# A side schedule re-timed: the normalisation two slots later, half of the GELU matrices one slot later, a flip and a projection shifted, and the query rotation rearranged

## The chip, the cores and the metric

The program runs on one core of one Trainium2 chip. Its time is the device time of one launch in microseconds (us); the kernel before took 6043.84 us in the median of three runs (6041.26 to 6050.09). A core has a matrix engine (TensorE, PE in the profile, its weight loads PEld), VectorE (DVE), ScalarE (ACT), GpSimd (POOL) and the queue that issues DMAs (SyncE, SP). Each works through its own instructions strictly in order, and they wait for each other by semaphores.

## The reference

Eight blocks follow each other (a transformer stack with expert layers and recurrences between them). Only the first is touched: six layers over a batch of 16 items of 56 query rows by 128 features, 16 heads of 8, a context of 1500 keys.

```python
for i in range(NL):                          # NL = 6
    xn = _adaln(x, noise_emb, n1_w[i], n1_b[i])          # (x - mean) / std, scaled and shifted per item
    q, k, v = jnp.split(xn @ qkv_w[i].T, 3, axis=-1)
    a = _attn(_rope(q), _rope(k), v, src_mask) @ so_w[i].T      # self attention, 56 keys
    x = x + a
    xn = _adaln(x, noise_emb, n2_w[i], n2_b[i])
    q = _rope(xn @ cq_w[i].T)
    k = _rope(context @ ck_w[i].T)                              # cross attention, 1500 keys
    v = context @ cv_w[i].T
    a = _attn(q, k, v, ctx_mask) @ co_w[i].T
    x = x + a
    xn = _adaln(x, noise_emb, n3_w[i], n3_b[i])
    h = jax.nn.gelu(xn @ f1_w[i].T + f1_b[i], approximate=False)
    x = x + (h @ f2_w[i].T + f2_b[i])
# _rope(x) = [x1 * cos - x2 * sin, x1 * sin + x2 * cos], x1 and x2 the halves of a head
```

## The kernel before

**Slots.** The cross attention is the bulk of the block. It is cut into 6 x 16 = 96 units s (layer and batch item), and each unit into 12 key tiles kt of 125 keys: one pair (s, kt) is a slot. In each slot TensorE forms the scores of 16 heads in two halves (L1561), ScalarE takes their exponentials (L2067), and TensorE multiplies them with the values (L1587). Beside that a slot forms part of the scores of a later unit a first time (L1575), of which VectorE takes row maxima (L1940).

**Keys and queries.** Ahead of its unit each third of a key block (500 keys) is made by two matmuls (L1601) into a PSUM bank. VectorE turns it (a shuffle of the halves, L1821) and multiplies it with the cosines (L1822); the second one frees the bank. GpSimd then multiplies by the sines (L2087), adds (L2091), and, since the scores run in three bfloat16 parts, forms the rest (L2094, after ScalarE's high part, L1966) and the low part (L2097, after ScalarE's middle part, L1970). DMAs carry the parts to the key stack. In `key_gpsimd` these steps stand at the slots +1, +2 and +3 of the key block (`late`). The query goes the same way (L2105, L1976).

**The side work.** Everything else of the layer (the self attention, the norms, the MLP) is for half a batch (8 units) at once and is spread over the 96 slots of these units. Such a stretch is a phase, numbered ph from -1 to 12, and t = 0 to 95 counts its slots. Phases -1 and 12 are the run-up and the end, with little or no scoring. What stands where is set by tables: `T_NORM` (start of the three norms), `T_UP` (which of the four MLP matrices, with their GELUs, at which t), `T_DOWN`, `T_ROPE` (three rotations of queries and keys), `T_SV`, `T_SELF` (eight self attentions, each from t = a: scores at a, transposes `st` at a+2, weighing `sw` a+3, turn a+4, flip a+5, and for each second one a projection at a+7). A norm that starts at t = at has its mean at +0, its variance at +2, and its application by GpSimd in two halves of three instructions each (`norm_gpsimd`), at +3 and +4 (called in `gpsimd`); the matrices that read it stand at +7.

**The banks.** All side work on TensorE writes to three PSUM banks (4, 6, 7), taken in turn by the class `Banks`. A user's bank is its rank in one list, modulo three. The list is written by `fixed_order` (key, value, turn, flip, project, rows), `phase_order` and `self_weigh_order`, slot by slot. A matmul waits until the user three ranks ahead has been read (`side.emptied(...)`, `side.before`), and its reader waits for `side.filled`. So a user that moves within the list shifts the bank of each user that it passes.

**The engines' programs.** For each slot TensorE, VectorE and ScalarE call first `fixed_*`, then `phase_*`; the activation table of ScalarE holds exponential and logarithm (`LN_EXP`), and the GELU needs another, so that ScalarE loads tables around it (L2022, L2025). In a slot GpSimd calls the norm halves before or after the key steps as `gpsimd` has them.

Of the kernel before, what the change touches and what calls it, by code (L numbers as in the profile page):

```python
# [113 lines left out]
def by_batch(a):  # L114
    return a.rearrange("p (b s) -> p b s", s=S)
# [1127 lines left out]
T_UP, T_DOWN, T_ROPE, T_SV = {13: (0, 1, 2, 3)}, 15, {23: 0, 24: 1, 71: 2}, 24  # L1243
# [10 lines left out]
class Block0:  # L1254
# [12 lines left out]
    def __init__(self, k):  # L1267
        self.k = k
        ev = k.events
        with ExitStack() as st:  # L1270
# [24 lines left out]
            self.largest = sb("row_max", [QC, PAIRS, 3])  # L1295
            self.m_part = sb("neg_max_parts", [QC, WIDE], BF16)[:, :]
# [70 lines left out]
        self.rope_turned = Ordered(k, "l0_rope_turned", [(*key, i) for key in ropes for i in range(2)])  # L1367
# [33 lines left out]
    def fixed_order(self, s, kt):  # L1401
# [7 lines left out]
        if 1 <= s <= NS and kt == 3:  # L1409
            order.append(("flip", s - 1))  # L1410
# [11 lines left out]
    def phase_order(self, ph, t):  # L1422
# [16 lines left out]
        if nxt:  # L1439
            for i, a in enumerate(T_SELF(ph)):  # L1440
# [8 lines left out]
                if t == a + 7 and i % 2 == 1:  # L1449
                    order.append(("sproject", ph, i // 2))  # L1450
# [141 lines left out]
    def fixed_tensor(self, e, s, kt):  # L1592
# [27 lines left out]
        if 1 <= s <= NS and kt == 3:  # L1620
# [38 lines left out]
    def phase_tensor(self, e, ph, t):  # L1659
# [48 lines left out]
        for i, a in enumerate(T_SELF(ph)):  # L1708
# [39 lines left out]
            if t == a + 7 and i % 2 == 1:  # L1748
# [29 lines left out]
    def max_parts_vector(self, e, s):  # L1778

        side, key = self.side, ("rows", s)  # L1780
        neg, m = side.bank(*key)[0:QC, BANK - PAIRS:BANK], self.m_part[:, 1:1 + 3 * PAIRS].rearrange(
            "q (p j) -> q p j", j=3)
        e.wait_ge(side.emptied(*key), side.before(*key))
# [56 lines left out]
    def phase_vector(self, e, ph, t):  # L1840
# [18 lines left out]
        if t in T_ROPE:  # L1859
# [4 lines left out]
            bk = side.bank(*key)[:, 0:HALF]  # L1864
# [4 lines left out]
            if n == 1:  # L1869
                e.wait_ge(self.roped.sem, self.roped(ph, 0))  # L1870
            e.scalar_tensor_tensor(out=by_batch(o), in0=by_batch(bk), scalar=scale, in1=cs, op0=ALU.mult,
                                   op1=ALU.mult).then_inc(self.rope_turned.sem, 1)
            e.wait_ge(self.rope_turned.sem, self.rope_turned(ph, n, 0))
            e.stream_shuffle(bk, bk, OTHER_HALF).then_inc(self.rope_turned.sem, 1)
            e.wait_ge(self.rope_turned.sem, self.rope_turned(ph, n, 1))
            e.scalar_tensor_tensor(out=by_batch(bk), in0=by_batch(bk), scalar=scale, in1=sn, op0=ALU.mult,
                                   op1=ALU.mult).then_inc(self.rope_sin.sem, 1)
            e.wait_ge(self.rope_sin.sem, self.rope_sin(ph, n))
            e.tensor_tensor(o, bk, o, ALU.add).then_inc(self.roped.sem, 1)
            e.drain().then_inc(side.emptied(*key), 1)  # L1880
# [1801 lines left out]
```

## Time and profile before

| | |
|---|---|
| median of three runs (range) | 6043.84 us (6041.26 to 6050.09) |
| profiled execution: time, span | 6043.84 us, 6042.0 us |
| PE busy, share of the span, instructions | 5595.8 us, 93%, 55893 |
| PEld | 4177.1 us, 69%, 55893 |
| DVE | 3779.0 us, 63%, 8627 |
| ACT | 3230.0 us, 53%, 6405 |
| POOL | 2247.7 us, 37%, 2204 |

Shares are over the whole span of eight blocks. The span in 40 slices (each digit a tenth of the slice in which the engine is busy; PEclk is the granted clock of TensorE in tenths of full speed) shows the first block in slices 2 to 20:

```profile
PE   5899999999999999999799999998799999989997
ACT  1566666666766766667543344443333333324764
POOL 4666666666666666656200000000011111156440
PEclk7999999999999999999898999999799999998998
```

The costliest groups of the page (line, engine, operation, tensors with partitions x elements, count, then busy us and mean ns, then the engine's idle time just before them and what ended most of it) are the inner loop of the slots. VectorE's maxima waited for TensorE 170 us, ScalarE's exponentials 515 us:

```profile
L1940 DVE TENSOR_REDUCE row_max<-psum 112x1 f32<-112x500 f32 x2304 | 1443.3, 670 | 185.2 <-PE psum L1575 170.4
L2067 ACT ACTIVATE weights<-psum 125x448 f32<-125x448 f32 x2304 | 1140.8, 541 | 521.2 <-PE psum L1561 514.6
L1575 PE MATMUL psum<-key_stack,query_stack 97*128 97x500 bf16 x2304 | 874.6, 380 | 111.0 <-DMA query_stack<-query_parts 51.1
L1561 PE MATMUL psum<-query_stack,key_stack 121*128 121x112 bf16 x9216 | 837.6, 213 | 33.2 <-ACT weights L2067 27.9
```

### The profile page before, as it was taken

The page shows a single profiled execution, that of the slowest core. Times are in us where ns is not written, and L with a number is a line of the kernel's source. Part 1 is how long each engine was busy: PE and PEld are TensorE (multiplying, and loading weights), DVE is VectorE, ACT ScalarE, POOL GpSimd, SP SyncE. Part 2 cuts the span into 40 slices and gives each one's busy share as a digit, 9 for nine tenths or more (in the row PEclk, how much of TensorE's full clock was granted, in tenths as well). Part 3 has the DMA queues.
Part 4 walks back from the last instruction along what each step waited for, and adds up shares of the span by engine and source line. Part 5 has one row for each costly group of instructions (what it writes and reads, how often), then busy time and mean ns, then how long its engine had stood idle before and what let it go on. Part 6 is the DMA issues. An engine that isn't in the chain of part 4 may idle for free.

```text
span 6042.0 us, 140669 instructions
## 1 busy us (share of the span) xinstructions
PE 5595.8 (93%) x55893; PEld 4177.1 (69%) x55893; DVE 3779.0 (63%) x8627; ACT 3230.0 (53%) x6405; POOL 2247.7 (37%) x2204
## 2 busy tenths in 40 slices
PE   5899999999999999999799999998799999989997
PEld 4667667677676676776457778776477777756984
DVE  3888888887887888888553444444544444444553
ACT  1566666666766766667543344443333333324764
POOL 4666666666666666656200000000011111156440
PEclk7999999999999999999898999999799999998998
DMA  2776776776767767768400100001000000030000
GB/s 63 120 118 106 119 120 104 120 116 107 125 110 115 121 109 116 121 107 130 92 11 10 42 32 32 30 29 33 11 11 16 11 16 11 11 105 24 1 1 25
DMA packets 396485, 407.85 MB, mean 68 GB/s; under 512 B 125575, under 2 KB 372946, under 8 KB 393786
## 3 DMA queue, kind: packets, MB, share of 16 engines
q1 hardware_dynamic: 395834, 398.85, 37.6%
q8 instruction: 447, 7.32, 0.6%
q14 instruction: 204, 1.67, 0.1%
HBM read 158.00 MB, written 0.46 MB: 26 GB/s over the span
## 4 chain that ended last, share of the span: by engine, by line
PE 62%; POOL 8%; SPq 7%; DVE 7%; issue 7%; ACT 5%; DMA 3%; POOLq 1%; DVEq 0%; ACTq 0%
PE psum L2276 11%; PE psum L2243 10%; PE psum L1575 5%; PE psum L1587 4%; PE psum L2288 4%; PE psum L1561 4%; SPq L1475 4%; POOL slot_context L3476 3%; PE psum L1723 2%; PE psum L1609 2%; PE psum L1601 2%; SPq L1493 2%; PE psum L416 2%; PE psum L430 2%; DVE row_max L1940 2%
## 5 line engine op out<-in xcount | busy, mean ns | idle before, releaser
L1940 DVE TENSOR_REDUCE row_max<-psum 112x1 f32<-112x500 f32 x2304 | 1443.3, 670 | 185.2 <-PE psum L1575 170.4
L2067 ACT ACTIVATE weights<-psum 125x448 f32<-125x448 f32 x2304 | 1140.8, 541 | 521.2 <-PE psum L1561 514.6
L1575 PE MATMUL psum<-key_stack,query_stack 97*128 97x500 bf16 x2304 | 874.6, 380 | 111.0 <-DMA query_stack<-query_parts 51.1
L1561 PEld LDWEIGHTS psum<-query_stack,key_stack 121*128 121x128 bf16 x9216 | 654.1, 99 | 370.9 <-issue 184.6
L1561 PE MATMUL psum<-query_stack,key_stack 121*128 121x112 bf16 x9216 | 837.6, 213 | 33.2 <-ACT weights L2067 27.9
L2356 DVE TENSOR_REDUCE l_stat<-psum 128x1 f32<-128x1500 f32 (+1 forms) x224 | 391.7, 1749 | 544.9 <-PE psum L2243 544.9
L2276 PE MATMUL psum<-l_ctx_v,l_turned 125*128 125x128 f32 x5376 | 713.7, 281 | 16.4 <-ACT l_turned L2314 12.2
L2276 PEld LDWEIGHTS psum<-l_ctx_v,l_turned 125*128 125x128 f32 x5376 | 643.1, 191 | 59.2 <-ACT l_turned L2314 40.2
L1587 PE MATMUL psum<-weights,values 125*17 125x112 f32 x18432 | 553.9, 261 | 0.0
L1587 PEld LDWEIGHTS psum<-weights,values 125*17 125x17 f32 x18432 | 408.0, 97 | 144.1 <-issue 141.2
L2314 ACT ACTIVATE l_turned<-psum 125x512 f32<-125x512 f32 x448 | 251.3, 597 | 434.9 <-PE psum L2288 432.1
L2097 POOL TENSOR_TENSOR key_parts<-key_temp,key_parts 128x500 bf16<-128x500 f32 x288 | 327.2, 1136 | 420.0 <-ACT key_parts L1970 420.0
L2087 POOL TENSOR_TENSOR key_temp<-key_temp,rope_sin 128x500 f32<-128x500 f32 x288 | 360.4, 1252 | 280.3 <-DVE key_temp L1821 280.3
L2973 POOL MEMSET l_turned<- 125x128 f32 x2 | 0.4, 216 | 1169.1 <-DVE x_state L796 1169.1
L2288 PE MATMUL psum<-ident,l_weights 128*125 128x128 f32 (+1 forms) x2800 | 400.6, 276 | 19.4 <-ACT l_keys L2823 8.0
L2094 POOL TENSOR_TENSOR key_temp<-key_temp,key_parts 128x500 f32<-128x500 f32 x288 | 328.3, 1140 | 233.6 <-ACT key_parts L1966 233.6
L2288 PEld LDWEIGHTS psum<-ident,l_weights 128*125 128x125 f32 (+1 forms) x2800 | 348.8, 185 | 83.0 <-issue 39.4
L2091 POOL TENSOR_TENSOR key_temp<-key_temp 128x500 f32<-128x500 f32 x288 | 358.2, 1244 | 42.4 <-POOL key_temp L2087 1.7
L2339 ACT ACTIVATE l_weights<-psum,l_stat 128x1500 f32<-128x1500 f32 (+1 forms) x224 | 344.0, 1536 | 38.1 <-DVE l_stat L2356 38.1
L2837 POOL TENSOR_TENSOR l_ctx_v<-l_ctx_v,l_ctx_w 125x512 f32<-125x512 f32 x48 | 61.0, 1272 | 786.0 <-DVE l_ctx_v L2831 786.0
L1575 PEld LDWEIGHTS psum<-key_stack,query_stack 97*128 97x128 bf16 x2304 | 224.1, 97 | 173.4 <-DMA query_stack<-query_parts 72.5
L2243 PE MATMUL psum<-l_keys,l_q 128*128 128x389 f32 x896 | 314.9, 493 | 4.2 <-ACT l_weights L2339 3.6
(539 smaller groups left out, 10182.9 us busy)
## 6 DMA issues: line engine op xcount, KB each, us to landing
key_stack<-key_parts SPq DMA_DIRECT2D x1728, 125.0 KB, 4.6
ctx_t<-in_ctxT SPq DMA_DIRECT2D x96, 750.0 KB
l_ctx_v<-in_ctxV SPq DMA_DIRECT2D x32, 750.0 KB
query_stack<-query_parts SPq DMA_DIRECT2D x576, 28.0 KB, 3.5
l_ctx_t<-in_ctxT SPq DMA_DIRECT2D x16, 750.0 KB
slot_context<-in_ctxV SPq DMA_DIRECT2D x16, 750.0 KB
key_stack<-ctx_mask_rows SPq DMA_DIRECT2D x576, 3.9 KB
sm_w<-in_sm_w SPq DMA_DIRECT2D x3, 2048.0 KB
```

The lines of the kernel that those rows point to most:

```text
L1561: mm = e.matmul(self.k.psum[:, h, (p % 4) * QC:(p % 4 + 1) * QC], ks[:, at:at + 128], q[:, p * QC:(p + 1) * QC])
L1575: e.matmul(self.k.psum[:, 2 + n % 2, 0:500], q[0:ROWS_MAX, p * QC:p * QC + 128], ks[0:ROWS_MAX, p, c * 500:(c + 1) * 500]).then_inc(self.m ...
L1587: mm = e.matmul(self.k.psum[32 * j:32 * j + 17, 5, g * QC:(g + 1) * QC], v[:, kt, p, :], w[:, p * QC:(p + 1) * QC], start=kt == 0 and g == ...
L1940: e.tensor_reduce(self.largest[:, i % PAIRS, i // PAIRS:i // PAIRS + 1], k.psum[0:QC, 2 + i % 2, 0:500], AX.X, ALU.max, negate=True).then_ ...
L2067: e.activation(half(self.p[kt % RING_P], h), self.k.psum[0:KN, h, 0:HALF], ACT.Exp).then_inc(self.exped.sem, 1)
L2087: e.tensor_tensor(tm[:, 1, :], tm[:, 1, :], self.sin[:, c * 500:(c + 1) * 500], ALU.mult).then_inc(self.key_turned_sin.sem, 1)
L2091: e.tensor_tensor(tm[:, 0, :], tm[:, 0, :], tm[:, 1, :], ALU.add).then_inc(self.key_rotated.sem, 1)
L2243: mm = e.matmul(k.psum[:, c, 0:self.step], q[:, r * 128:(r + 1) * 128], self.keys(b)[:, c * self.step:(c + 1) * self.step])
L2276: mm = e.matmul(k.psum[:, 6, 0:128], pt[:, t, :], v[:, t, :], start=t == 0, stop=t == self.tiles - 1)
L2288: tr = e.transpose(bk[0:rows, t * 128:(t + 1) * 128], self.p[j % 2][:, c0:c0 + rows], k.ident[:, :])
L2339: e.activation(self.p[i % 2].rearrange("p (c n) -> p c n", c=self.n_s), k.psum[:, 0:self.n_s, 0:self.step], ACT.Exp, bias=stat[:, 1:2], ac ...
L2356: e.tensor_reduce(self.stat[i % 4][:, 1:2], k.psum[:, 0:self.n_s, 0:self.step], AX.XY, ALU.max, negate=True).then_inc(self.max_ready.sem, 1)
```

## The change

Six edits, all in the first block:

1. `T_UP` spreads the four MLP matrices over two slots (two at t = 13, two at t = 14), and the exponential's table is loaded back after the second and after the fourth GELU.
2. The negated row maximum and what is subtracted from it lie in a tile of their own in SBUF instead of a corner of a side bank, and VectorE no longer waits for that bank before it.
3. The cross attention's head flip moves from kt = 3 to kt = 4, on TensorE, on ScalarE and in the list of banks.
4. The self attention's projection moves from a+7 to a+6, on TensorE, on VectorE and in the list of banks.
5. The rotation first shuffles from PSUM into the idle half of the scratch `k.sq`, then multiplies from PSUM by the cosines, which frees the bank; the product with the sines and the sum read and write SBUF, and the drain is gone.
6. GpSimd's two halves of a norm move from +3 and +4 to +5 and +6.

```diff
-T_UP, T_DOWN, T_ROPE, T_SV = {13: (0, 1, 2, 3)}, 15, {23: 0, 24: 1, 71: 2}, 24
+T_UP, T_DOWN, T_ROPE, T_SV = {13: (0, 1), 14: (2, 3)}, 15, {23: 0, 24: 1, 71: 2}, 24
...
+            self.neg = sb("neg_max", [QC, PAIRS])[:, :]
...
-        self.rope_turned = Ordered(k, "l0_rope_turned", [(*key, i) for key in ropes for i in range(2)])
+        self.rope_turned = Ordered(k, "l0_rope_turned", ropes)
...
# fixed_order; the same in fixed_tensor and fixed_scalar
-        if 1 <= s <= NS and kt == 3:
+        if 1 <= s <= NS and kt == 4:
             order.append(("flip", s - 1))
...
# phase_order; the same in phase_tensor and phase_vector
-                if t == a + 7 and i % 2 == 1:
+                if t == a + 6 and i % 2 == 1:
                     order.append(("sproject", ph, i // 2))
...
# max_parts_vector
-        side, key = self.side, ("rows", s)
-        neg, m = side.bank(*key)[0:QC, BANK - PAIRS:BANK], self.m_part[:, 1:1 + 3 * PAIRS].rearrange(
-            "q (p j) -> q p j", j=3)
-        e.wait_ge(side.emptied(*key), side.before(*key))
+        neg, m = self.neg, self.m_part[:, 1:1 + 3 * PAIRS].rearrange("q (p j) -> q p j", j=3)
...
# phase_vector, rotation
-            bk = side.bank(*key)[:, 0:HALF]
+            bk, other = side.bank(*key)[:, 0:HALF], half(k.sq, 1 - c)
...
+            e.stream_shuffle(other, bk, OTHER_HALF).then_inc(self.rope_turned.sem, 1)
             e.scalar_tensor_tensor(out=by_batch(o), in0=by_batch(bk), scalar=scale, in1=cs, op0=ALU.mult,
-                                   op1=ALU.mult).then_inc(self.rope_turned.sem, 1)
-            e.wait_ge(self.rope_turned.sem, self.rope_turned(ph, n, 0))
-            e.stream_shuffle(bk, bk, OTHER_HALF).then_inc(self.rope_turned.sem, 1)
-            e.wait_ge(self.rope_turned.sem, self.rope_turned(ph, n, 1))
-            e.scalar_tensor_tensor(out=by_batch(bk), in0=by_batch(bk), scalar=scale, in1=sn, op0=ALU.mult,
+                                   op1=ALU.mult).then_inc(side.emptied(*key), 1)
+            e.wait_ge(self.rope_turned.sem, self.rope_turned(ph, n))
+            e.scalar_tensor_tensor(out=by_batch(other), in0=by_batch(other), scalar=scale, in1=sn, op0=ALU.mult,
                                    op1=ALU.mult).then_inc(self.rope_sin.sem, 1)
+            e.wait_ge(side.emptied(*key), side.after(*key))
             e.wait_ge(self.rope_sin.sem, self.rope_sin(ph, n))
-            e.tensor_tensor(o, bk, o, ALU.add).then_inc(self.roped.sem, 1)
-            e.drain().then_inc(side.emptied(*key), 1)
+            e.tensor_tensor(o, o, other, ALU.add).then_inc(self.roped.sem, 1)
...
# phase_scalar
-            if f == 3:
+            if f % 2 == 1:
                 e.preload_act_table_set(LN_EXP)
...
# gpsimd
-                    if layer is not None and t - at - 3 in range(2):
-                        self.norm_gpsimd(e, name, ph, layer, t - at - 3)
+                    if layer is not None and t - at - 5 in range(2):
+                        self.norm_gpsimd(e, name, ph, layer, t - at - 5)
```

Lines move with the edits: L1561 becomes L1562 and so on for TensorE; in the programs of ScalarE and GpSimd all lines are three lower.

The first place is GpSimd around the cross norm of phase 5. `x_normed` is the normalised state, three instructions a half; `key_temp` and `key_parts` are the steps of key blocks. Before:

```order
L2097 TENSOR_TENSOR key_parts<-key_temp,key_parts 128x500
L2121 TENSOR_TENSOR x_normed<-ln_deviation 128x224
L2124 TENSOR_TENSOR x_normed<-x_normed,adaln_scale_shift 128x224
L2126 TENSOR_TENSOR x_normed<-x_normed,adaln_scale_shift 128x224
L2121 TENSOR_TENSOR x_normed<-ln_deviation 128x224
L2124 TENSOR_TENSOR x_normed<-x_normed,adaln_scale_shift 128x224
L2126 TENSOR_TENSOR x_normed<-x_normed,adaln_scale_shift 128x224
L2087 TENSOR_TENSOR key_temp<-key_temp,rope_sin 128x500
L2091 TENSOR_TENSOR key_temp<-key_temp 128x500
L2094 TENSOR_TENSOR key_temp<-key_temp,key_parts 128x500
L2097 TENSOR_TENSOR key_parts<-key_temp,key_parts 128x500
L2105 TENSOR_TENSOR query_block<-l_q,head_parity 128x112
```

After:

```order
L2094 TENSOR_TENSOR key_parts<-key_temp,key_parts 128x500
L2084 TENSOR_TENSOR key_temp<-key_temp,rope_sin 128x500
L2088 TENSOR_TENSOR key_temp<-key_temp 128x500
L2118 TENSOR_TENSOR x_normed<-ln_deviation 128x224
L2121 TENSOR_TENSOR x_normed<-x_normed,adaln_scale_shift 128x224
L2123 TENSOR_TENSOR x_normed<-x_normed,adaln_scale_shift 128x224
L2091 TENSOR_TENSOR key_temp<-key_temp,key_parts 128x500
L2118 TENSOR_TENSOR x_normed<-ln_deviation 128x224
L2121 TENSOR_TENSOR x_normed<-x_normed,adaln_scale_shift 128x224
L2123 TENSOR_TENSOR x_normed<-x_normed,adaln_scale_shift 128x224
L2094 TENSOR_TENSOR key_parts<-key_temp,key_parts 128x500
L2102 TENSOR_TENSOR query_block<-l_q,head_parity 128x112
```

Both halves stood ahead of the next key block's first product; now that block's two products come first, then half one, the rest, half two and the low part.

The second place is TensorE in slot 44 of phase 3. L1601 is the key block (`l_w_context`), L1732 the seven transposes of the self weights (`self_p`) into two banks, four and three, and L1753 the projection (`self_attended`). Before:

```order
L1561 MATMUL psum<-query_stack,key_stack 128x112 x4
L1575 MATMUL psum<-key_stack,query_stack 128x500
L1601 MATMUL psum<-ctx_t,l_w_context 128x500
L1732 MATMUL psum<-ident,self_p 56x128 x7
L1561 MATMUL psum<-query_stack,key_stack 128x112 x4
L1575 MATMUL psum<-key_stack,query_stack 128x500
L1561 MATMUL psum<-query_stack,key_stack 128x112 x4
L1575 MATMUL psum<-key_stack,query_stack 128x500
L1587 MATMUL psum<-weights,values 17x112 x16
L1652 MATMUL psum<-self_pt,self_v 17x112 x8
L1753 MATMUL psum<-self_attended,l_w_attend 128x112
L1561 MATMUL psum<-query_stack,key_stack 128x112 x4
```

After:

```order
L1562 MATMUL psum<-query_stack,key_stack 128x112 x4
L1576 MATMUL psum<-key_stack,query_stack 128x500
L1602 MATMUL psum<-ctx_t,l_w_context 128x500
L1754 MATMUL psum<-self_attended,l_w_attend 128x112
L1733 MATMUL psum<-ident,self_p 56x128 x7
L1562 MATMUL psum<-query_stack,key_stack 128x112 x4
L1576 MATMUL psum<-key_stack,query_stack 128x500
L1562 MATMUL psum<-query_stack,key_stack 128x112 x4
L1576 MATMUL psum<-key_stack,query_stack 128x500
L1588 MATMUL psum<-weights,values 17x112 x16
L1653 MATMUL psum<-self_pt,self_v 17x112 x8
L1562 MATMUL psum<-query_stack,key_stack 128x112 x4
```

In these rows a slot begins with its scores (L1561). The projection has moved from the end of slot 45 to slot 44, between the key block and the transposes. With three banks in turn, the key block, the projection and the first four transposes now take one each, and the last three transposes take the key block's again.

The third place is ScalarE at the MLP matrices of a phase. The GELUs write `l_qd`, the exponentials `weights`. Before:

```order
L1957 ACTIVATE sums<-psum 128x224
L2022 ACT_TABLE_LOAD
L2022 ACTIVATE l_qd<-psum,l_bias 128x448 x4
L2025 ACT_TABLE_LOAD
L2067 ACTIVATE weights<-psum 125x448 x2
L1966 ACTIVATE key_parts<-key_temp 128x500
L1976 ACTIVATE query_parts<-query_block 128x112
L1987 ACTIVATE values<-psum 125x32x16
L2067 ACTIVATE weights<-psum 125x448 x2
```

After:

```order
L1954 ACTIVATE sums<-psum 128x224
L2019 ACT_TABLE_LOAD
L2019 ACTIVATE l_qd<-psum,l_bias 128x448 x2
L2022 ACT_TABLE_LOAD
L2064 ACTIVATE weights<-psum 125x448 x2
L1963 ACTIVATE key_parts<-key_temp 128x500
L1973 ACTIVATE query_parts<-query_block 128x112
L1984 ACTIVATE values<-psum 125x32x16
L2019 ACT_TABLE_LOAD
L2019 ACTIVATE l_qd<-psum,l_bias 128x448 x2
L2022 ACT_TABLE_LOAD
L2064 ACTIVATE weights<-psum 125x448 x2
```

Two of the GELUs, with a table load ahead and one behind, now stand after the next slot's exponentials and after the copies for key (`key_parts`), query (`query_parts`) and values.

## Rows read from the trace of the kernel before

**Rows 1.** A window: from:to, us, busy of PE PEld DVE ACT POOL, PEclk, DMA share, GB/s.

```profile
182.00:2924.00 2742.00, 2605.29 (x37126) 1896.23 (x37126) 2261.74 (x5128) 1862.88 (x4042) 1699.67 (x1693) 1.00 0.73 116
```

**Rows 2.** TensorE's waits, 200 to 2800: total us, times, longest.

```profile
PE psum L1575 <- DMA query_stack<-query_parts: 41.6, 28, 3.4
PE psum L1575 <- DVE row_max L1940: 30.1, 44, 1.4
PE psum L1561 <- ACT weights L2067: 25.3, 32, 1.0
...
PE psum L1575 <- DMA key_stack<-key_parts: 3.2, 11, 0.3
```

**Rows 3.** Timeline, MLP norm, phase 4: start, us, engine, line, tile, [idle before <-releaser].

```profile
1145.22 0.66 POOL L2121 TENSOR_TENSOR x_normed<-ln_deviation 128x224 f32<-128x224 f32 x1
...
1147.12 1.14 POOL L2094 TENSOR_TENSOR key_temp<-key_temp,key_parts 128x500 f32<-128x500 f32 x1
...
1148.30 0.62 ACT L1970 ACTIVATE key_parts<-key_temp 128x500 bf16<-128x500 f32 x1 [0.51 <-POOL key_temp L2094]
...
1151.46 3.52 PE L1681 MATMUL psum<-x_normed,l_w_mlp 128*128 128x448 f32 x8
```

**Rows 4.** The same timeline, tables and GELUs of ScalarE.

```profile
1151.97 1.28 ACT L2022 ACT_TABLE_LOAD   x1
...
1153.27 2.38 ACT L2022 ACTIVATE l_qd<-psum,l_bias 128x448 f32<-128x448 f32 x4
...
1155.66 1.28 ACT L2025 ACT_TABLE_LOAD   x1
...
1157.56 0.37 PE L1561 MATMUL psum<-query_stack,key_stack 121*128 121x112 bf16 x4 [0.45 <-ACT weights L2067]
...
1158.52 0.60 ACT L1987 ACTIVATE values<-psum 125x512 f32<-125x512 f32 x1
```

**Rows 5.** Timeline, phase 5, norm and rotation of the cross attention, then a later slot.

```profile
1541.06 0.73 DVE L1821 STREAM_SHUFFLE key_temp<-psum 128x500 f32<-128x500 f32 x1
...
1544.68 1.24 POOL L2087 TENSOR_TENSOR key_temp<-key_temp,rope_sin 128x500 f32<-128x500 f32 x1
...
1547.07 1.02 PE L1698 MATMUL psum<-x_normed,l_w_attend 128*128 128x448 f32 x2
1547.35 0.62 ACT L1966 ACTIVATE key_parts<-key_temp 128x500 bf16<-128x500 f32 x1 [3.12 <-POOL key_temp L2091]
...
1549.03 0.36 PE L1561 MATMUL psum<-query_stack,key_stack 121*128 121x112 bf16 x4 [0.94 <-ACT weights L2067]
...
1551.62 0.38 PE L1575 MATMUL psum<-key_stack,query_stack 97*128 97x500 bf16 x1 [0.57 <-DVE row_max L1940]
...
1570.58 0.38 PE L1575 MATMUL psum<-key_stack,query_stack 97*128 97x500 bf16 x1 [1.38 <-DMA query_stack<-query_parts]
```

**Rows 6.** The same timeline, first and last instruction of the rotation on VectorE.

```profile
1548.12 0.62 DVE L1871 SCALAR_TENSOR_TENSOR l_q<-psum,rope_cos 128x448 f32<-128x448 f32 x1 [0.38 <-PE psum L1698]
...
1550.12 0.62 DVE L1879 TENSOR_TENSOR l_q<-psum,l_q 128x448 f32<-128x448 f32 x1
```

**Rows 7.** Timeline, slot 44 of phase 3.

```profile
1003.82 1.00 PE L1601 MATMUL psum<-ctx_t,l_w_context 128*128 128x500 f32 x2
...
1004.67 0.93 PE L1732 MATMUL psum<-ident,self_p 128*56 128x128 f32 x7
...
1005.43 0.36 PE L1561 MATMUL psum<-query_stack,key_stack 121*128 121x112 bf16 x4
1005.49 0.66 DVE L1822 TENSOR_TENSOR key_temp<-psum,rope_cos 128x500 f32<-128x500 f32 x1
...
1007.62 0.47 PE L1753 MATMUL psum<-self_attended,l_w_attend 128*128 128x112 f32 x2
```

**Rows 8.** TensorE's timeline in phase 5.

```profile
1382.08 0.60 PE L1575 MATMUL psum<-key_stack,query_stack 97*128 97x500 bf16 x1 [2.01 <-DMA query_stack<-query_parts]
```

**Rows 9.** The window behind that wait, columns as in rows 1.

```profile
1381.80:1385.20 3.40, 3.12 (x17) 2.75 (x18) 1.36 (x2) 1.05 (x2) 1.57 (x3) 0.50 1.08 138
```

More of the change, by code:

```diff
@@ L1619, in fixed_tensor @@
             tr.then_inc(side.filled, 1)
-        if 1 <= s <= NS and kt == 3:
+        if 1 <= s <= NS and kt == 4:
             key = ("flip", s - 1)
@@ L1747, in phase_tensor @@
                 e.transpose(side.bank(*key)[:, 0:TALL], self.so_tall, k.ident[0:TALL, 0:TALL]).then_inc(side.filled, 1)
-            if t == a + 7 and i % 2 == 1:
+            if t == a + 6 and i % 2 == 1:
                 key = ("sproject", ph, i // 2)
@@ L1900, in phase_vector @@
                 self.divide(e, ("sturn", ph, i), self.sinv, self.so, self.s_inverted, self.s_inverted(ph, i))
-            if t == a + 7 and i % 2 == 1:
+            if t == a + 6 and i % 2 == 1:
                 key, m = ("sproject", ph, i // 2), c * (BH // 2) + i // 2
@@ L1989, in fixed_scalar @@
                          ACT.Copy).then_inc(side.emptied(*key), 1)
-        if 1 <= s <= NS and kt == 3:
+        if 1 <= s <= NS and kt == 4:
             key, b = ("flip", s - 1), s - 1
```

## The prediction

> **What bounds the kernel now.** I read the engines' busy shares first, then the window of the stage that the change touches, then what TensorE waits for there, then single slots in order of time. All edits lie in the first block, whose scoring runs from 182 to 2924 us. TensorE is busy 2605.3 of those 2742.0 us [rows 1]; the other engines leave far more. So the stage is TensorE's instruction stream laid end to end, plus 136.7 us of holes: about 11.6 us in each of its nearly twelve phases of 96 slots (a slot is one of the 12 key tiles of one batch item). Its waits are short: for query rows that a DMA brings, for VectorE's row maxima, for ScalarE's exponentials, now and then for key rows [rows 2]. Three things follow. An edit can win at most what it takes out of those holes. A faster side engine wins nothing elsewhere. And every new wait of TensorE counts in full unless the next hole swallows it. In all of the stage TensorE has no wait of weight for a normalised state, for a key block's bank or for a head flip, the three things that the change re-times.
>
> **The later normalisation, MLP.** GpSimd now does its two halves (three instructions each) in slots +5 and +6 instead of +3 and +4, and the consumer's slot is still +7. GpSimd works in order, so both halves stand behind all three steps of the key block (two products and sums, rest, low part). Before, in phase 4: a half takes 1.90 us (1145.22 to the next start at 1147.12), and TensorE starts the up-projection at 1151.46 without waiting [rows 3]. Now: ScalarE's middle copy waited 0.51 us for GpSimd's rest and could start at 1147.79; with its 0.62 us the low part runs from 1148.45 to 1149.6. Then two halves, 3.85 us: 1153.5. TensorE comes at 1151.46, so it waits 2.05 us. Eleven phases inside the stage: **+22.6 us**. The key block is ready 1.7 us earlier, but TensorE did not wait for it here.
>
> **The split up-projection.** Two of the four matrices move a slot later, and the load back to the exponential's table now follows each pair, so there are four loads a phase instead of two. Before, ScalarE loads for 1.28 us, four GELUs take 2.38, the load back ends at 1156.94, and TensorE loses 0.45 us in the next slot and some 0.5 in the fourth matrix [rows 4]. Now, counted from the first matrix: load back done at 3.43, the next slot's two exponentials, key, query and value copies at 5.6 (the value copy of 1158.52 ends 2.2 us after the load did [rows 4]); the fourth matrix needs the bank of that value copy. TensorE has by 4.35 done two matrices (half of 3.52), the next slot's own matmuls (about 1.7) and the third matrix (0.88), so it waits 1.3 us. Against 0.95 lost before: +0.3 us, 11 phases, 3.3 us. Behind the scoring the last phase has nothing beside it: two more loads, 2.6 us. Together **+5.9 us**; bounds -0.95 (no wait left) and +2.6 (both loads in full) per phase.
> The GELUs start at 1153.27, 0.02 us behind the end of the load (1151.97 + 1.28), and TensorE has its exponential 0.6 us behind the end of the load back, which is about the length of that exponential [rows 4]: a load costs its 1.28 us and no more.
> The Trainium skill ("ScalarE: Activation LUTs", What ACT_TABLE_LOAD costs) puts a drain of about 1.38 us on ScalarE beside each load; this case's trace does not agree [rows 4]. By that page an estimate would be 24 more loads at 1.38, 33 us more of ScalarE's time, and 9 us more in the sum if a quarter of it reached TensorE.
>
> **The later normalisation, before the rotations.** Self and cross attention of each phase have the same four lines of order; I take the cross one. Before: both halves ran ahead of the next key block, whose shuffle had ended at 1541.79; that block started only at 1544.68, and TensorE lost 0.94 us to exponentials stuck behind it [rows 5]. Now: the key block's two products (1.25 each) run 1541.8 to 1544.35, half one to 1546.25, rest (1.14) to 1547.4, half two to 1549.35. TensorE stood ready at 1547.07: it waits 2.35 us. The 0.94 us is no gain, because behind the rotation VectorE sets the pace: TensorE waits 0.57 us for a row maximum anyway [rows 5], and the self site ends likewise. What is late next is therefore VectorE's chain, which is shifted whole and shortened only by the quicker rotation.
> The rotation: four instructions from 1548.12 to 1550.74, about 0.67 apart [rows 6], become four, of which the second and third no longer wait for the one before, and the drain goes. A like-sized instruction out of SBUF is unseen beside GpSimd; I take equal durations and 0.25 us saved each, bounds 0 and 0.6.
> Self: two rotations in the chain, 2.35 - 0.5 = 1.85, times 11 phases, **+20.4 us**. Cross: 2.35 - 0.25 = 2.1, less what later holes swallow. GpSimd and the DMAs behind it are no later than now, so the wait for the query's rows, 1.38 us in this phase [rows 5], shrinks; it is not there in each phase (waits of this kind are 28 in the stage, at several places [rows 2]), so I count 0.8 of it, and 0.2 of the key rows' wait of 0.3 [rows 2]: 1.1 left, times 11, **+12.1 us**. The same order in the run-up delays the first keys: +3 us, bounds 0 and 5.
>
> **The moved flip and projection.** They change nothing that TensorE waits for, but each takes one of three rotating banks. In slots 28, 36, 40, 44 and 52 of a phase one bank user now stands between the key block and the turned self weights, so the last three transposes (in slot 52 the first four) land in the key block's own bank and must wait until VectorE has multiplied it. Slot 44: key product at 1003.82, transposes from 1004.67, next scores at 1005.43, hence 0.11 each and the fifth at 1005.11; VectorE is done with the bank at 1005.49 + 0.66 = 1006.15 [rows 7]. That is 1.05 us, +0.1 for the signal, minus what now stands in between, 0.15 (flip) or 0.25 (projection, half of the 0.47 in [rows 7]): 1.0, 0.9, 1.0, 0.9. Slot 52: 1.05 + 0.44 + 0.1 - 0.4 = 1.2. Sum 5.0 us a phase, no hole behind to swallow it: **+55 us** over 11 phases; bounds 3.5 and 6.
> The maxima's negation moves from PSUM to SBUF: five tiny instructions, no wait of TensorE behind them: 0, bounds -0.1 and +0.05 a row.
>
> **The clock.** After a hole of 2.01 us the granted clock fell to 0.50 (1.2 of 2.4 GHz) for the 3.4 us from 1381.8 on [rows 8, 9], 1.7 us of progress lost. There will be 33 new holes of 2.05 to 2.35 us. None or all give 0 to 56 us; half of them, and half of the loss hidden behind VectorE's chain: **+15 us**.
> The sum is 22.6 + 5.9 + 20.4 + 12.1 + 3 + 55 + 15 = 134 us on the profiled execution, whose span is 6042.0 and whose time, 6043.84, is also the median. 6178; I round down to **6172 us**, as overlaps are likelier to eat than to add.
>
> **Rivals.** (a) Half of the bank waits and norm waits are swallowed by holes I counted as local (0.9 us in slots 34, 46): 6044 + 68 = 6112. For: ScalarE and GpSimd get time in each. Against: those holes hang on the same slot's copies. (b) GpSimd and VectorE disturb each other: two of a rotation's instructions now read two SBUF operands; if each waits on the mean half of a 1.25 us GpSimd instruction at GpSimd's busy share of 62% (1699.7 of 2742.0 us [rows 1]), that is 0.39, times 2, times 33 = 25 us more: 6200. No instruction pair of the kind in this block shows it or excludes it.
> The Trainium skill ("SBUF — State Buffer", Who interferes with whom) says that a VectorE instruction with two SBUF inputs and a GpSimd one that reads SBUF exclude each other for their whole length; rival (b) is that rule, and no row here bears on it.
> (c) The other side, faster: the later halves win. If they are done before TensorE reaches the rotation, the 0.94 us here and its twin at the self site, the DMA's 0.8 and three rotations' 0.25 go: -3.4 times 11 = -37, and without the bank waits 6007. It decides from GpSimd's low part ending 2.4 us sooner than I have it; against it stand 7.5 us of GpSimd work between 1541.8 and the rotation. (d) The change does not move the banks as I counted them, and the transposes find another bank: 6172 - 55 = 6117. Its chance stands with (a)'s. Against it: the bank of each user is its rank in one list, and I counted it through a phase.
>
> **Chances.** As worked out 0.63, its own range 6130 to 6215; (a) and (d) 0.17; (b) 0.12; (c) 0.08, of which half ends under 6032. A measurement here tells apart about 0.2% (12 us). Range 6090 to 6220. Faster 0.05, same 0.03, slower 0.92.
>
> **What would show it.** TensorE's wait list gains three entries that it does not have: matmuls of the up-projection and of the rotation for GpSimd's normalised state (near 68 us together, [rows 2] had none) and transposes for VectorE's key product (near 55 us). ScalarE's wait for the key sum at the rotation, 3.12 us [rows 5], is down to a few tenths. Table loads in the stage double. Wrong would be: no wait for the normalised state, or transposes that start as early as 0.85 us after the key product as in [rows 7].

## The result: 3.7% slower, and outside the range

The changed kernel takes 6272.59 us in the median of four runs (6262.12 to 6280.45), the kernel before 6046.97 us beside it (6041.26 to 6052.37): the ratio is 1.0372, 95% interval 1.0353 to 1.0391, or some 226 us. The prediction said 6172 us (6090 to 6220). Its sign was right and so were most of its waits; it had 128 us of the 226. The profiled execution took 6286.42 us (span 6284.6), that of before 6043.84.

The stage from the first exponentials of the scoring to the last is 2781.0 us long before and 3011.4 us now. A window over it, first of the kernel before, then of the changed one (from:to, length, busy of PE PEld DVE ACT POOL, PEclk, DMA share, GB/s):

```profile
182.00:2963.00 2781.00, 2641.00 (x37764) 1921.47 (x37768) 2280.28 (x5170) 1889.24 (x4097) 1699.67 (x1693) 1.00 0.72 114
```

```profile
182.60:3194.00 3011.40, 2716.51 (x37765) 1973.53 (x37769) 2391.54 (x5170) 1936.02 (x4119) 1704.42 (x1693) 0.97 0.67 106
```

These two rows split the loss. TensorE's holes grow from 140.0 to 294.9 us, by 155. Its busy time grows by 75.5 us with the same matmuls: that is the clock, which is down to 0.97 on the mean. In the clock record the time at 0.50 in the stage is 26 us before and 172 us now, and half of the difference, 73 us, is nearly all of the longer busy time. VectorE is busy 111 us longer with as many instructions.

TensorE's waits in the changed kernel (200 to 2980 us), beside [rows 2]:

```profile
PE psum L1576 <- DVE row_max L1937: 65.7, 44, 4.0
PE psum L1733 <- DVE key_temp L1820: 47.2, 55, 1.1
PE psum L1639 <- DVE neg_max_parts L1791: 46.3, 35, 2.2
PE psum L1576 <- DMA query_stack<-query_parts: 38.3, 30, 3.4
PE psum L1699 <- POOL x_normed L2123: 25.7, 22, 1.2
PE psum L1682 <- POOL x_normed L2123: 15.9, 10, 1.8
PE psum L1682 <- ACT values L1984: 15.3, 10, 2.4
```

The second, fifth, sixth and seventh rows are the waits of the prediction: transposes for the key block's bank, matmuls for the normalised state, the fourth MLP matrix for the value copy. The normalised state has 41.6 us where the prediction had near 68: the rotations wait 1.17 us each, not 2.35, for a reason that the experiments show below. The third row is new and was not forecast, and the first has doubled from 30.1 us. The banks can be seen in one place (slot 36 of phase 4, the case of [rows 7]): key product, projection, four transposes, then 0.73 us of waiting for VectorE's product, and three more:

```profile
1315.92 1.40 PE L1602 MATMUL psum<-ctx_t,l_w_context 128*128 128x500 f32 x2
1317.16 0.37 PE L1754 MATMUL psum<-self_attended,l_w_attend 128*128 128x112 f32 x2
1317.37 0.60 PE L1733 MATMUL psum<-ident,self_p 128*56 128x128 f32 x4
1318.70 0.51 PE L1733 MATMUL psum<-ident,self_p 128*56 128x128 f32 x3 [0.73 <-DVE key_temp L1820]
```

**What was not forecast.** The chain that negates the row maximum, slot 34 of phase 4, with GpSimd beside it (timeline of both engines):

```profile
1302.18 1.25 POOL L2088 TENSOR_TENSOR key_temp<-key_temp 128x500 f32<-128x500 f32 x1 [0.43 <-POOL key_temp L2084]
...
1302.64 0.18 DVE L1783 TENSOR_REDUCE neg_max<-row_max 112x8 f32<-112x24 f32 x1
...
1302.85 0.61 DVE L1785 CAST neg_max_parts<-neg_max 112x8 bf16<-112x8 f32 x1
...
1303.38 1.69 POOL L2160 TENSOR_TENSOR l_qd<-l_q,head_of_feature 128x896 f32<-128x896 f32 x1
1303.50 1.60 DVE L1787 TENSOR_TENSOR neg_max<-neg_max,neg_max_parts 112x8 f32<-112x8 f32 x1
...
1305.03 1.13 POOL L2091 TENSOR_TENSOR key_temp<-key_temp,key_parts 128x500 f32<-128x500 f32 x1
1305.13 1.07 DVE L1789 CAST neg_max_parts<-neg_max 112x8 bf16<-112x8 f32 x1
1306.23 0.18 DVE L1791 TENSOR_TENSOR neg_max_parts<-neg_max,neg_max_parts 112x8 bf16<-112x8 f32 x1
...
1306.55 0.28 PE L1639 MATMUL psum<-ident_bf,neg_max_parts 112*72 112x112 bf16 x1 [2.23 <-DVE neg_max_parts L1791]
```

Read the ends. The CAST of eight columns ends at 1303.46, GpSimd's sum at 1303.43. GpSimd has begun its next instruction, which ends at 1305.07; the TENSOR_TENSOR ends at 1305.10. The second CAST ends at 1306.20, GpSimd's third instruction at 1306.16. A chain that takes 1.02 us where nothing holds it takes 3.8 us, because between two of VectorE's short instructions GpSimd gets in with its next one. Over the whole execution 94 of the 96 first CASTs start beside a GpSimd instruction, and all 94 end 32 to 41 ns behind its end; before, with the chain in PSUM, none of the 96 took over 0.18 us. The reduction (L1783) is never longer than 0.18 us, whatever GpSimd does.

The rotation of the keys, same phase, in the same way; two instructions that take 0.63 and 0.62 us in PSUM ([rows 6] has the like of the second) take 1.64 and 1.92:

```profile
1274.15 1.24 POOL L2088 TENSOR_TENSOR key_temp<-key_temp 128x500 f32<-128x500 f32 x1
1274.23 1.64 DVE L1873 SCALAR_TENSOR_TENSOR ln_square<-ln_square,rope_sin 128x448 f32<-128x448 f32 x1
...
1275.35 2.06 POOL L2160 TENSOR_TENSOR l_qd<-l_q,head_of_feature 128x896 f32<-128x896 f32 x1
1275.97 1.92 DVE L1877 TENSOR_TENSOR l_k<-l_k,ln_square 128x448 f32<-128x448 f32 x1
1277.82 2.61 DVE L1937 TENSOR_REDUCE row_max<-psum 112x1 f32<-112x500 f32 x4
1278.63 0.37 PE L1576 MATMUL psum<-key_stack,query_stack 97*128 97x500 bf16 x1 [4.02 <-DVE row_max L1937]
```

It holds the other way round too: GpSimd's instruction at 1275.35 begins while VectorE has the sine product and takes 2.06 us instead of 1.69. TensorE waits 4.02 us for the row maxima queued behind the rotation, once a phase.

The two rotations of queries are not held in this kernel: each takes 2.42 us instead of 2.62, near the 0.25 us that the prediction saved; the rotation of the keys takes 4.74 us instead of 2.61, in all eleven phases.

The Trainium skill ("SBUF — State Buffer", Who interferes with whom) states this rule: VectorE and GpSimd share a port pair as an exclusive lock; an instruction with two SBUF inputs against a reading GpSimd instruction takes it, a copy in a two-port mode takes it, a reduction never does. The durations agree in all three (1.60 us, 0.61 to 1.07 us, 0.18 us); no view shows which mode a CAST ran in.

### The profile page after: what moved, and what is told of

It is laid out like the page before. It is cut to its first block, busy times and chain, and to the rows that moved or that the text cites. A ratio compares the mean times of both kernels' runs of the same rounds, so it can differ in the third digit from the quotient of the medians.

```text
span 6284.6 us, 140597 instructions
## 1 busy us (share of the span) xinstructions
PE 5678.5 (90%) x55893; PEld 4239.4 (67%) x55893; DVE 3890.6 (62%) x8627; ACT 3279.5 (52%) x6429; POOL 2252.9 (36%) x2204
## 4 chain that ended last, share of the span: by engine, by line
PE 62%; DVE 9%; POOL 9%; issue 7%; SPq 5%; ACT 5%; DMA 3%; POOLq 1%; DVEq 0%; ACTq 0%
PE psum L2273 10%; PE psum L2240 9%; PE psum L1576 5%; PE psum L1562 4%; PE psum L1588 4%; PE psum L2285 4%; PE psum L1610 3%; PE psum L1724 3%; POOL slot_context L3473 3%; SPq L1476 3%; PE psum L1602 2%; PE psum L416 2%; PE psum L430 2%; DVE row_max L1937 2%; SPq L1494 1%
## 5 line engine op out<-in xcount | busy, mean ns | idle before, releaser
L1576 PE MATMUL psum<-key_stack,query_stack 97*128 97x500 bf16 x2304 | 889.4, 387 | 146.0 <-DVE row_max L1937 70.9
L1562 PEld LDWEIGHTS psum<-query_stack,key_stack 121*128 121x128 bf16 x9216 | 658.7, 100 | 347.9 <-issue 160.9
L1562 PE MATMUL psum<-query_stack,key_stack 121*128 121x112 bf16 x9216 | 849.3, 215 | 7.4 <-ACT weights L2064 2.1
L2273 PE MATMUL psum<-l_ctx_v,l_turned 125*128 125x128 f32 x5376 | 713.6, 281 | 16.1 <-ACT l_turned L2311 12.1
L1610 PEld LDWEIGHTS psum<-l_w_context,ctx_t 128*125 128x125 f32 x2304 | 316.8, 198 | 10.4 <-issue 1.3
```

The source lines that it names most:

```text
L1562: mm = e.matmul(self.k.psum[:, h, (p % 4) * QC:(p % 4 + 1) * QC], ks[:, at:at + 128], q[:, p * QC:(p + 1) * QC])
L1576: e.matmul(self.k.psum[:, 2 + n % 2, 0:500], q[0:ROWS_MAX, p * QC:p * QC + 128], ks[0:ROWS_MAX, p, c * 500:(c + 1) * 500]).then_inc(self.m ...
L1610: mm = e.matmul(side.bank(*key)[0:KN, i * 128:(i + 1) * 128], self.ctx_t[b % 2][:, t * KN:(t + 1) * KN], self.wk[b // B % 2][:, 1, :])
L2273: mm = e.matmul(k.psum[:, 6, 0:128], pt[:, t, :], v[:, t, :], start=t == 0, stop=t == self.tiles - 1)
```

## The experiments

Each kernel is the kernel before with the named edits, unless it says otherwise. "Holes" is the stage's length less TensorE's busy time, both from a window over the stage as above; "slow" the time at 0.50 of the clock in it. Differences are against before (2781.0, 140.0, 2641.0, 26). The ratio compares medians; the other columns come from one profiled execution of each kernel, that of before at 6043.84 us, where the medians beside the runs were 6047 to 6052, so they can differ from the ratio by some 10 us. Half of "slow" agrees with the longer busy time within 12 us in each row; where the rest comes from (11 us in `without_rope`, 8 in `neg_reduce`) stays open.

| kernel | edits | ratio (95%) | stage | holes | busy | slow |
|---|---|---|---|---|---|---|
| changed | 1-6 | 1.0372 (1.0353-1.0391) | +230 | +155 | +76 | +146 |
| neg_alone | 2 | 1.0229 (1.0214-1.0244) | +142 | +58 | +84 | +170 |
| neg_reduce | 2, CASTs as reductions | 1.0057 (1.0040-1.0074) | +41 | +23 | +19 | +22 |
| rope_alone | 5 | 1.0097 (1.0063-1.0131) | +68 | +33 | +35 | +82 |
| banks_alone | 3, 4 | 1.0087 (1.0070-1.0104) | +60 | +49 | +11 | +9 |
| norm_alone | 6 | 1.0136 (1.0121-1.0151) | +90 | +52 | +38 | +84 |
| norm4_alone | 6 at +4 | 1.0062 (1.0047-1.0077) | +41 | +11 | +30 | +65 |
| up_alone | 1 | 1.0034 (1.0022-1.0046) | +17 | +15 | +2 | +5 |
| timing_only | 1, 3, 4, 6 | 1.0257 (1.0242-1.0273) | +148 | +105 | +43 | +80 |
| without_neg | 1, 3-6 | 1.0294 (1.0279-1.0309) | +174 | +123 | +51 | +107 |
| without_rope | 1-4, 6 | 1.0345 (1.0324-1.0366) | +201 | +132 | +69 | +115 |
| short_steps | none, GpSimd cut | 0.9958 (0.9944-0.9972) | -19 | -33 | +15 | +15 |
| short_neg | 2, GpSimd cut | 0.9980 (0.9969-0.9991) | +0 | -23 | +23 | +32 |

**The negation alone.** The diff is that of `max_parts_vector` in the change.

> The kernel before, with only the maximum's negation moved to SBUF (edit 2). Theory P (VectorE and GpSimd exclude each other): the first CAST takes the rest of the GpSimd instruction that runs when it starts, on average 0.5 to 0.6 us over its 0.17, the whole chain of five about 1.0 us longer; TensorE's transposes of neg_max_parts wait near 40 us in the stage; 6044 + 45 = 6090 us (6070 to 6110). Rival Q (the chain is late only because the norm's halves moved): CAST near 0.17 us, 6044 within 12 us.

Measured 1.0229, 135 us between the medians: Q falls, and P's mechanism stands with three times its price. The five instructions' durations (min/median/max ns):

```profile
L1783 DVE TENSOR_REDUCE neg_max<-row_max x91: 167/178/180, 205.1 to 2994.4; 112x8 f32<-112x24 f32 x91
L1785 DVE CAST neg_max_parts<-neg_max x91: 322/768/1476, 205.3 to 2994.6; 112x8 bf16<-112x8 f32 x91
L1787 DVE TENSOR_TENSOR neg_max<-neg_max,neg_max_parts x91: 166/168/1600, 206.1 to 2995.4; 112x8 f32<-112x8 f32 x91
L1789 DVE CAST neg_max_parts<-neg_max x91: 177/179/1067, 206.3 to 2995.6; 112x8 bf16<-112x8 f32 x91
L1791 DVE TENSOR_TENSOR neg_max_parts<-neg_max,neg_max_parts x91: 176/179/1161, 206.5 to 2995.8; 112x8 bf16<-112x8 f32 x91
```

The holes it makes are 58 us, near P; the other 84 are slow clock, which P left out. In slots 34 and 46 of a phase TensorE waits 1.8 and 1.7 us for the chain (mean of twelve phases), and these slots are 2.5 us longer; in slots 22 and 70 it waits 1.2 us each.

**The CASTs as reductions.**

```diff
-        e.tensor_copy(m[:, :, 0], neg).then_inc(self.negated.sem, 1)
+        e.tensor_reduce(m[:, :, 0], neg.unsqueeze(2), AX.X, ALU.min).then_inc(self.negated.sem, 1)
...
-        e.tensor_copy(m[:, :, 1], neg).then_inc(self.negated.sem, 1)
+        e.tensor_reduce(m[:, :, 1], neg.unsqueeze(2), AX.X, ALU.min).then_inc(self.negated.sem, 1)
```

> As neg_alone, but both CASTs are made as a TENSOR_REDUCE over one element, so that of the five instructions only the two TENSOR_TENSORs read two SBUF operands and none is a plain copy. Theory P1 (only the copy and the two-operand forms wait for GpSimd; the first of them in the chain pays for the running GpSimd instruction): both reductions take 0.17 to 0.2 us, the first TENSOR_TENSOR takes the rest of GpSimd's instruction, 0.5 to 0.8 us, and the time is that of neg_alone or up to 20 us less. P2 (any SBUF operand beside GpSimd is slow): the reductions grow too. P3 (only the copy waits): all five near 0.18 us and the time within 12 us of before.

```profile
L1785 DVE TENSOR_REDUCE neg_max_parts<-neg_max x95: 168/169/171, 200.8 to 2985.7; 112x8 bf16<-112x8 f32 x95
L1787 DVE TENSOR_TENSOR neg_max<-neg_max,neg_max_parts x95: 166/550/1258, 201.0 to 2985.9; 112x8 f32<-112x8 f32 x95
L1789 DVE TENSOR_REDUCE neg_max_parts<-neg_max x95: 167/168/172, 201.6 to 2986.1; 112x8 bf16<-112x8 f32 x95
L1791 DVE TENSOR_TENSOR neg_max_parts<-neg_max,neg_max_parts x95: 176/389/1414, 201.8 to 2986.3; 112x8 bf16<-112x8 f32 x95
```

P1 is right on each instruction: the same data in the same tile, read by a reduction, costs nothing beside GpSimd, and the wait passes to the next TENSOR_TENSOR. P2 and P3 fall. P1's time was wrong: with two instructions instead of four that can meet GpSimd the cost is 34 us, not 115 to 135. What fell most is the slow clock, from 170 us to 22.

**GpSimd's steps cut, without and with the negation in SBUF.**

```diff
-                e.tensor_tensor(tm[:, 0, :], tm[:, 0, :], tm[:, 1, :], ALU.add).then_inc(self.key_rotated.sem, 1)
+                e.tensor_tensor(tm[:, 0, 0:4], tm[:, 0, 0:4], tm[:, 1, 0:4], ALU.add).then_inc(self.key_rotated.sem, 1)
...
-                e.tensor_tensor(part[:, 2, :], tm[:, 1, :], part[:, 1, :], ALU.subtract).then_inc(self.key_lo.sem, 1)
+                e.memset(part[:, 2, :], 0).then_inc(self.key_lo.sem, 1)
```

> The kernel before with GpSimd's key steps cut short: sine product, sum and rest work on 4 of 500 columns, and the low part is a MEMSET (it only writes SBUF). So the scores are not the reference's. It is the control for the next one. GpSimd's busy time in the stage falls from 1700 us to some 700; TensorE's stream is the same, its waits for key rows and exponentials behind the rotation shrink: 5990 to 6045 us.

> short_steps with the negation in SBUF (edit 2). Theory P: the chain now starts beside no GpSimd instruction that reads much of SBUF, so CAST and TENSOR_TENSOR take 0.17 to 0.2 us in most of the 96 chains, and the time is that of short_steps within 15 us, where the same edit on the kernel before cost 135 us. A CAST that begins beside the MEMSET tells whether a writing instruction holds it as well. Rival (SBUF tiles are slower for these instructions by themselves, or the missing wait for the bank moves something): 60 to 135 us over short_steps.

The control took 6023.61 us, the other 6041.42: the edit costs 18 us here and 135 us with GpSimd's work in place. Its first CAST:

```profile
L1785 DVE CAST neg_max_parts<-neg_max x95: 177/179/547, 194.3 to 2938.7; 112x8 bf16<-112x8 f32 x95
```

So the chain is slow because of what GpSimd does beside it, not because of SBUF. The 18 us are 3 over what P allowed; 44 of the 96 first CASTs still start beside what is left of GpSimd's work, most of them just before its end, and 11 are held, for 0.53 to 0.55 us in all. No CAST met a MEMSET, so whether a GpSimd instruction that only writes holds it stays open.

**The rotation alone.** The diff is that of the rotation in the change.

> The kernel before, with only the rotation rearranged through SBUF (edit 5). Theory P: one of the three sine products and the sum of the key rotation meet a GpSimd instruction and grow by 0.9 and 1.3 us, the other ones keep 0.62; TensorE waits about 1.5 us a phase more for row maxima behind the key rotation: 6044 + 15 = 6059 us (6045 to 6075). Rival Q (equal durations, 0.25 us saved for each rotation): 6036 to 6044 us.

Measured 1.0097, about 60 us (from 40 to 80 by the interval): Q falls, P is again right in kind and low in price. Slot 26, from its first score to that of the next slot, grows from 5.47 to 10.15 us on the mean of eleven phases. TensorE waits 3.8 us there, where it waited 1.41. The list of waits puts nine of these eleven under key rows:

```profile
PE psum L1575 <- DMA key_stack<-key_parts: 35.0, 9, 3.9
```

But the timeline shows P's wait, for the row maximum behind the rotation (phase 4):

```profile
1218.58 1.92 DVE L1879 TENSOR_TENSOR l_k<-l_k,ln_square 128x448 f32<-128x448 f32 x1
1220.42 2.77 DVE L1939 TENSOR_REDUCE row_max<-psum 112x1 f32<-112x500 f32 x4
1221.23 0.45 PE L1575 MATMUL psum<-key_stack,query_stack 97*128 97x500 bf16 x1 [3.89 <-DMA key_stack<-key_parts]
```

In each of the eleven phases TensorE starts 0.15 us behind the end of the first of these row maxima, as it does in the kernel before and in the changed kernel; a signal of the key rows' DMA falls within 0.1 us of that start in ten of them, eight times after it, so the list's name for these waits is not what ended them. P also left out that the last sum of the query rotations meets GpSimd here: it takes 1.6 us in 20 of 22, and such a rotation 3.4 us instead of 2.62. In the changed kernel, with the norm's halves later, it is not held.

**Flip and projection alone.** `kt == 3` to `kt == 4` and `a + 7` to `a + 6`, as in the change.

> The kernel before, with only the flip and the projection moved (edits 3 and 4). Theory as in the prediction: the self attention's transposes wait 0.7 to 1.1 us for VectorE's key product in five slots of a phase, 47 us in the stage, the slots grow by 5.0 us a phase: 6044 + 57 = 6101 us (6085 to 6115). Rival (other holes swallow half): 6072 us.

Measured 1.0087, 6102.67 us where 6101 was expected, or 51 us over the runs of before beside it (6051.9) where 57 was. The wait is the one forecast, 55 times (five a phase), and the rival falls:

```profile
PE psum L1732 <- DVE key_temp L1822: 47.1, 55, 1.1
```

**The later halves alone, by two slots and by one.** `t - at - 3` to `t - at - 5`, and to `t - at - 4`.

> The kernel before, with only the norm's halves two slots later (edit 6). Theory as in the prediction: TensorE waits for the normalised state 2.05 us at the MLP matrices and 2.35 us at both rotations, 22.6 + 20.4 + 12.1 + 3 us and some 10 us of slower clock: 6044 + 68 = 6112 us (6090 to 6130). Rival (the waits are 1.05 to 1.6 us, as in the changed kernel, and are so by themselves): 6044 + 35 = 6079 us.

```profile
PE psum L1698 <- POOL x_normed L2126: 50.9, 22, 2.3
PE psum L1681 <- POOL x_normed L2126: 19.9, 11, 1.8
```

Measured 1.0136, some 82 us. The waits are those of the prediction: 22 of 2.31 us at the rotations (2.35 forecast), 11 of 1.81 at the MLP matrices (2.05); the rival falls. The holes of the stage grow by 52 us, where the prediction had 22.6 + 20.4 + 12.1 = 55.1. The slow clock is 38 us, not 10.

> The kernel before, with the norm's halves one slot later instead of two (+4, +5). If GpSimd's order alone decides: at the MLP matrices the second half ends near 1151.3 on the timeline of before, where TensorE comes at 1151.46, and at the rotations the key block's first product runs between the halves, which end at 1547.2 where TensorE comes at 1547.07; no wait over 0.3 us for the normalised state and 0.5 us less wait for exponentials at both rotations: 0.998 to 1.000 of before. Rival (any later half costs): 1.005 or more.

```profile
PE psum L1575 <- DVE row_max L1940: 44.3, 43, 2.0
...
PE psum L1681 <- POOL x_normed L2126: 9.3, 10, 0.9
...
PE psum L1698 <- POOL x_normed L2126: 4.8, 21, 0.2
```

Wrong: 1.0062. It is the rival's figure. At the rotations the wait is 0.2 us as expected, but at the MLP matrices 0.9, and what is won on the exponentials' 0.94 us [rows 5] comes back elsewhere: TensorE's wait for exponentials falls from 25.3 us [rows 2] to 5.1, that for row maxima rises from 30.1 to 44.3, and 14.1 us for the normalised state are new. The sum of the holes is only 11 us more, and 30 us are slow clock.

**The split up-projection alone.** The diff is that of `T_UP` and of the load back.

> The kernel before, with only the split up-projection (edit 1). As in the prediction: +3.3 us in the scoring, +2.6 us behind it, 6044 to 6060 us, within 0.3% of before. Rival (the wait for the value copy in the fourth matrix, 15.3 us in the stage of the changed kernel, is all new time): 1.0025 to 1.004.

```profile
PE psum L1681 <- ACT values L1987: 19.9, 11, 2.2
```

Measured 1.0034, 20 us: the rival. The fourth matrix waits 1.8 us a phase (1.3 forecast), and what was to be saved against it is not there: slots 13 to 15 together are 1.4 us longer, where the prediction had 0.3.

**All but the two edits to SBUF.**

> The changed kernel with the negation back in PSUM and the rotation as before (edits 1, 3, 4 and 6 stay, 2 and 5 undone). Theory P (the terms of the prediction stand, what it left out is VectorE against GpSimd): the sum of the prediction without the faster rotations, 6172 to 6190 us, that is 1.021 to 1.024 of before; CAST and TENSOR_TENSOR of the negation all 0.17 to 0.18 us. Rival (the excess lies in the moves themselves, which hurt each other): above 6230 us.

Measured 6200.64 us, 1.0257, some 10 us over the range of the theory and 30 below the rival. These four edits are the sum that the prediction worked out. The rotations wait for the normalised state as forecast, 2.32 us each:

```profile
PE psum L1698 <- POOL x_normed L2126: 51.0, 22, 2.3
```

**The changed kernel without one of them.**

> The changed kernel with only the negation back in PSUM (all edits but 2). If the edits' costs add up, edit 2 is worth 135 us here too: 6138 us. If they share holes (a later normalisation lets GpSimd and VectorE come to other phases, and the time at slow clock does not add): between the 6201 of timing_only and 6273, I take 6240 us; clock in the stage slow for 120 us or less instead of 172.

> The changed kernel with only the rotation as before (all edits but 5). Additive: 6272 - 60 = 6212 us. With shared holes: slot 26, where TensorE waited 3.61 us for VectorE behind the key rotation, loses 2.5 us of it, 27 us in the stage and 10 of clock: 6235 us.

6227.71 and 6259.64 us. The two edits cost 72 us on top of the others (6272.59 - 6200.64), where each alone costs 135 and 60 on the kernel before: costs are shared. The negation is worth 45 us in company with the rotation and 59 without it; the rotation 13 and 27, of which the 13 are no more than the noise of the two kernels (1.0372 and 1.0345, each within 0.002). Two places show how costs are shared. In slot 46 TensorE waits 1.84 us for the chain in neg_alone and 0.14 in the changed kernel (mean of eleven phases), where earlier waits have moved the engines against each other. And with the negation in SBUF TensorE waits for the chain in slots 22 and 70, one slot ahead of the rotations, 1.0 and 1.1 us; GpSimd works on meanwhile, and the wait for the normalised state in slots 23 and 71 is down from 2.32 us (timing_only, without_neg) to 1.17 (changed, without_rope). That is 25 us of 22 waits that the two edits have in common.

## Why the prediction was wrong, step by step

- **What bounds the stage** (TensorE laid end to end plus its holes): right. Every loss was found as a hole or as longer busy time, and the latter is slow clock within 12 us.
- **Later halves**: right. Alone 2.31 and 1.81 us a wait for 2.35 and 2.05, holes +52 for 55.1. In the changed kernel the rotations wait 1.17 us, since the chain's new wait stands ahead of them.
- **Split up-projection**: the wait was right in its cause, the term mis-sized: 20 us for 5.9. The step that failed is the 0.95 us "lost before", of which 0.5 was put on the fourth matrix; [rows 4] do not show that loss, and the waits before for it are 1.1 us in all.
- **Moved flip and projection**: right. 47 us of waits, 51 us alone (55 forecast).
- **The quicker rotation**: wrong in sign. It takes 2.13 us more for the keys instead of 0.25 us less, which is rival (b), held at 0.12; for the queries it takes 0.20 us less, as forecast. Rival (b) priced all 33 rotations at 25 us; the edit measured 13 to 27 us beside the others. But only one rotation of three waits in the changed kernel, and for 2.3 us instead of 0.8, so that this price is near by chance.
- **The negation** "no wait of TensorE behind them: 0": this step failed. It is the dearest of all edits alone. TensorE's transposes (L1639) do wait for it, 46.3 us in all, and the edit costs 135 us alone and 45 to 59 beside the others. The bounds of -0.1 to +0.05 us a row looked at the moved data and at the removed wait, not at what GpSimd does while the chain reads SBUF; rival (b) was applied to the rotation only, though CAST and TENSOR_TENSOR of the negation have the same operands.
- **The clock** at +15 us: mis-sized. The four edits that were summed rightly bring 43 us, all six 76. Half of the new holes and half of their loss was the guess; of 34 holes over 1.9 us that the changed kernel has between 190 and 3150 us, 24 have a stretch at 0.50 beginning within 9 us. One of them, behind the wait of 2.23 us shown above, is a window like that of [rows 9], 10.2 us long (5.1 us of work lost):

```profile
1306.50:1316.70 10.20, 10.15 (x74) 7.93 (x75) 6.02 (x14) 3.21 (x7) 1.46 (x2) 0.50 0.24 81
```

Added up: 134 of the prediction, with the clock at 43 instead of 15 and the table term at 20 instead of 6, would have been near 176; the four edits measured 153. Of the difference 9 us are terms summed too high (holes of 52 and 49 us for 55.1 and 55), 11 us are holes that the edits share (116 us in the three kernels that have them apart, 105 in timing_only), and 2 us are edit 1's clock, counted twice. The medians show no such sharing: 82, 51 and 20 us apart are 153 too. Rival (a), half of the waits swallowed, falls. The 72 us of VectorE against GpSimd are what put the result out of the range.

## What to carry to other kernels

Before data of a VectorE instruction are moved from PSUM to SBUF, look which engine runs beside it: against a busy GpSimd a copy or a two-operand instruction out of SBUF waits for the end of GpSimd's instruction, however small it is, and a chain of such instructions can wait once for each link. A reduction, or an operand left in PSUM, does not wait. Where TensorE is the bound, price a new hole of 2 us at more than its length: in these runs TensorE's longer busy time, most of it slow clock, came to between an eighth (edit 1) and nearly three times (edit 6 at +4) of the sum of the new holes. With GpSimd's steps cut it even grew by 15 us while the holes shrank by 33.

## What was not expected of the hardware

- The wait belongs to the instruction's form, not to the tile: 0.17 us for a reduction and 0.66 us on the mean (up to 1.48) for a CAST of the same 112x8 elements.
- The slow clock differs much more than the holes do. Edit 2 makes 58 us of holes and 170 us at 0.50; edits 3 and 4 make 49 us of holes, in waits of 0.7 to 1.1 us, and 9 us at 0.50. Each stretch at 0.50 that begins in the stage of the changed kernel, of neg_alone and of norm_alone begins within 5 us of the start of a hole of at least 1.29 us. Not each such hole has one: neg_alone has 79 of that length and 31 stretches.
- A table load had no drain beside it: it begins 0.02 us after ScalarE's instruction before it and takes 1.28 us, and the next begins 0.01 us behind its end (medians over all 153 loads of `up_alone`). The 24 more loads alone cost the kernel 20 us.
